# Attention over 4096 memory slots: the value matmuls on fp16 parts in place of fp32r parts

## The reference

```python
q = x @ Wq.T + bq
scores = einsum('bshd,hmd->bshm', q, memory_keys) / sqrt(128)
probs = softmax(scores, axis=-1)                 # over 4096 slots
mem_out = einsum('bshm,hmd->bshd', probs, memory_values)
x = layernorm(x + mem_out @ Wo.T + bo)
h = silu(x @ w1.T * s1) * (x @ w2.T * s2)
h = gelu(h @ h1.T * s_h1); h = gelu(h @ h2.T * s_h2)
out = layernorm(x + h @ w3.T * s3)
```

## Time and profile before

| | |
|---|---|
| median of 3 runs | 1188.73 us (1188.07 to 1192.92) |
| the profiled execution | 1189.26 us |
| its span, first to last instruction | 1187.5 us |
| attention block | until about 803 us |
| feed-forward block | the rest, some 384 us |
| mean granted TensorE clock | 0.978 |

### The profile page before, as it was taken

The page is one execution under the profiler, slowest core; times in us unless marked ns, Lnnn a source line. Parts: engine busy times, 40 slices in busy tenths (PEclk is TensorE's granted clock), DMA queues, the critical chain, the costliest instruction groups (busy, mean ns, idle before and its releaser), DMA issues. The chain is left out here.

```text
span 1187.5 us, 20054 instructions
## 1 busy us (share of the span) xinstructions
PE 1117.8 (94%) x5312; PEld 908.0 (76%) x5312; DVE 968.2 (82%) x1757; ACT 892.6 (75%) x1574; POOL 730.1 (61%) x612
## 2 busy tenths in 40 slices
PE   7799999999999999999999999753999999999996
PEld 6588788888888888888888887532688888888885
DVE  5888888888888888898898898464678878888875
ACT  5677787787878778787877877612788788888883
POOL 4388798889889888888888898882011112112110
PEclk9999999999999999999999999885999999999999
DMA  4878888888888888888888888812000100101000
GB/s 168 200 172 196 184 194 195 192 196 192 198 189 193 199 188 195 199 192 189 199 192 189 198 194 184 218 53 75 19 27 28 54 26 26 53 26 35 28 10 26
DMA packets 81922, 162.96 MB, mean 137 GB/s; under 512 B 19296, under 2 KB 44768, under 8 KB 81888
## 3 DMA queue, kind: packets, MB, share of 16 engines
q1 hardware_dynamic: 81888, 162.55, 57.5%
HBM read 19.87 MB, written 8.39 MB: 24 GB/s over the span
## 5 line engine op out<-in xcount | busy, mean ns | idle before, releaser
L259 POOL TENSOR_TENSOR pT<-slot_p,pT 128x512 fp32r<-128x512 f32 x512 | 653.4, 1314 | 108.8 <-ACT pT L298 108.8
L448 PE MATMUL o_ps<-pT,v_hi 128*128 128x512 f32 x1024 | 392.9, 406 | 21.6 <-POOL pT L259 21.0
L373 DVE TENSOR_SCALAR_CACHE_REDUCE rows<-s_ps 128x1024 f32<-128x1024 f32 x256 | 313.2, 1224 | 86.2 <-PE s_ps L421 77.0
L298 ACT ACTIVATE pT<-slot_p 128x512 fp32r<-128x512 f32 x512 | 297.5, 618 | 102.2 <-DMA slot_p<-rows 62.1
L342 DVE STREAM_TRANSPOSE rows<-rows 128x1024 f32<-128x1024 f32 x256 | 317.2, 1240 | 2.9 <-ACT rows L289 2.7
L289 ACT ACTIVATE rows<-rows,bias 128x1024 f32<-128x1024 f32 x256 | 292.3, 1142 | 9.0 <-DVE bias L379 6.2
L450 PE MATMUL o_ps<-pT,v_lo 128*128 128x256 f32 x1024 | 289.0, 282 | 0.0
L448 PEld LDWEIGHTS o_ps<-pT,v_hi 128*128 128x128 f32 x1024 | 195.1, 191 | 89.7 <-POOL pT L259 44.3
L419 PE MATMUL s_ps<-keys,q_buf 128*128 128x512 f32 x512 | 210.8, 412 | 9.7 <-DVE keys L169 5.2
L450 PEld LDWEIGHTS o_ps<-pT,v_lo 128*128 128x128 f32 x1024 | 195.8, 191 | 18.8
L798 PE MATMUL ring<-h_hi,keys 128*128 128x512 f32 x512 | 203.8, 398 | 1.9 <-DVE h_lo L705 1.6
(11 more groups left out here) (71 smaller groups left out, 1028.4 us busy)
## 6 DMA issues: line engine op xcount, KB each, us to landing
slot_p<-rows SPq DMA_DIRECT2D x1024, 128.0 KB, 2.3
x_in<-in_xT SPq DMA_DIRECT2D x32, 128.0 KB, 2.1
o_scratch<-o_sum SPq DMA_DIRECT2D x32, 128.0 KB, 1.9
o_in<-o_scratch SPq DMA_DIRECT2D x16, 256.0 KB, 2.8
x_in<-in_x SPq DMA_DIRECT2D x16, 256.0 KB, 3.1
out<-y_out SPq DMA_DIRECT2D x16, 256.0 KB, 2.3
slot_p<-in_kT SPq DMA_DIRECT2D x4, 512.0 KB, 6.1
slot_p<-in_vT SPq DMA_DIRECT2D x4, 512.0 KB, 9.2
```

Of the source, the lines that this page charges most:

```text
L259: nc.gpsimd.tensor_tensor(halves(s % RING, 1), slots_first(pp, s), halves(s % RING, 0).bitcast(FP32), ALU.subtract).then_inc(split, 1)
L298: nc.scalar.activation(halves(s % RING, 0), slots_first(pp, s), ACT.Copy).then_inc(highed, 1)
L373: nc.vector.tensor_scalar(row_piece(tile, k), s_ps[:, j % 2, :], 1.0, None, ALU.mult, ALU.max, accum_out=part_max[:, tile, k:k + 1]).then_ ...
L448: nc.tensor.matmul(o_ps[:, pp, :], v_hi[:, 2 * s + c, :], pT[:, s % RING, c, :], start=first, stop=False, skip_group_check=True)
```

## The change

`v_hi`, `v_lo` and `pT` become fp16. The values are multiplied by a power of two, so that fp16 can hold them: their largest magnitude is found on the chip, DVE by pieces of 1024 columns (`v_piece_max`), POOL across partitions, DVE turns it into `v_scale` and `v_unscale`. ACT copies the values to `v_raw` only, in frame 0; in steps 8 to 15 of frame 1 it writes the scaled `v_hi` and then scales `v_raw` in place. PE takes the two `v_lo` matmuls next to each other. The output is scaled back in the two instructions that form `o_sum`. The score matmuls and the feed-forward block stay as they are. The core of the diff:

```diff
-        v_hi = sb("v_hi", [P, SLOTS // P, P], FP32R)
-        v_lo = sb("v_lo", [P, SLOTS // P, P], FP32R)
+        v_hi = sb("v_hi", [P, SLOTS // P, P], FP16)
+        v_lo = sb("v_lo", [P, SLOTS // P, P], FP16)
...
-        pT = sb("pT", [P, RING, 2, 4 * P], FP32R)
+        pT = sb("pT", [P, RING, 2, 4 * P], FP16)
...
+            nc.gpsimd.memset(v_row_max[:, PIECES:PIECES + 1], V_LEAST).then_inc(v_least_ready, 1)
+            pool.wait_ge(v_row_maxed, PIECES + 1)
+            nc.gpsimd.partition_all_reduce(v_max[:, 0:1], v_row_max[:, PIECES + 1:], P, bass.bass_isa.ReduceOp.max).then_inc(v_maxed, 1)
             for n in range(HALVES):
                 pool.wait_ge(v_high, n + 1)
-                pool.wait_ge(v_copied, n + 1)
-                nc.gpsimd.tensor_tensor(half_piece(v_lo_flat, n), half_piece(v_raw, n), half_piece(v_hi_flat, n).bitcast(FP32),
+                pool.wait_ge(v_scaled, n + 1)
+                nc.gpsimd.tensor_tensor(half_piece(v_lo_flat, n), half_piece(v_raw, n), half_piece(v_hi_flat, n),
                                         ALU.subtract).then_inc(v_split, 1)
...
-                        nc.scalar.activation(half_piece(v_hi_flat, n), o_ps[:, n % 2, :], ACT.Copy).then_inc(v_high, 1)
...
+                    if is_step(f, 1) and t >= STEPS - HALVES:
+                        n = t - (STEPS - HALVES)
+                        if n == 0:
+                            act.wait_ge(v_scale_ready, 2)
+                        nc.scalar.activation(half_piece(v_hi_flat, n), half_piece(v_raw, n), ACT.Copy,
+                                             scale=v_scale[:, :]).then_inc(v_high, 1)
+                        act.wait_ge(v_high, n + 1)
+                        nc.scalar.activation(half_piece(v_raw, n), half_piece(v_raw, n), ACT.Copy,
+                                             scale=v_scale[:, :]).then_inc(v_scaled, 1)
...
+            def v_piece_max(n):
+
+                dve.wait_ge(v_copied, 2 * n + 2)
+                nc.vector.reduce_max(v_row_max[:, n:n + 1], piece(v_raw, n), AX.X, apply_absolute_value=True).then_inc(v_row_maxed, 1)
...
+                    if is_step(f, 0) and j > PIECES:
+                        v_piece_max(j - PIECES - 1)
+                    if is_step(f, 1) and j == 0:
+                        v_piece_max(PIECES - 1)
...
+                    if is_step(f, 1) and j == 3:
+                        dve.wait_ge(v_maxed, 1)
...
-                            if is_step(p, 0):
-                                pe.wait_ge(v_split, HALVES)
+                        if is_step(p, 0) and s % 2 == 0:
+                            pe.wait_ge(v_split, s // 2 + 1)
+                        nc.tensor.matmul(o_ps[:, pp, :], v_hi[:, 2 * s, :], pT[:, s % RING, 0, :],
+                                         start=s == 0, stop=False, skip_group_check=True)
                         for c in range(2):
...
+                            nc.tensor.matmul(o_ps[:, pp, 0:2 * P], v_lo[:, 2 * s + c, :], pT[:, s % RING, c, 0:2 * P],
+                                             start=False, stop=False, skip_group_check=True)
+                        nc.tensor.matmul(o_ps[:, pp, :], v_hi[:, 2 * s + 1, :], pT[:, s % RING, 1, :],
+                                         start=False, stop=s == STEPS - 1, skip_group_check=True).then_inc(pv_done, 1)
```

More of the change, by code:

```diff
@@ L22 @@
 FP16 = mybir.dt.float16
+I32 = mybir.dt.int32
 ALU = mybir.AluOpType
@@ L43 @@
 PV_LAG = 16
+V_TOP = 2.0 ** 14
+V_LEAST = 2.0 ** -100
 RING = 8
@@ L106, in attention @@
         table_spare = sb("exp_table_spare", [P, 1], FP32)
+        v_row_max = sb("v_row_max", [P, PIECES + 2], FP32)
+        v_max = sb("v_max", [P, 2], FP32)
+        v_scale = sb("v_scale", [P, 1], FP32)
+        v_unscale = sb("v_unscale", [P, 1], FP32)
         spare_half = slot_p[:, 1, :, :, :].rearrange("p a c t -> p (a c t)")
@@ L321, in frame @@
                         at_least(act, o_ready, f - 3)
-                        nc.scalar.activation(o_tmp[:, :], o_ps[:, 1 - par, 2 * P:], ACT.Copy).then_inc(o_half, 1)
+                        nc.scalar.activation(o_tmp[:, :], o_ps[:, 1 - par, 2 * P:], ACT.Copy,
+                                             scale=v_unscale[:, :]).then_inc(o_half, 1)
             frames(act, frame)
@@ L387, in frame @@
                         at_least(dve, o_stored, 16 * (f - 3))
-                        nc.vector.tensor_tensor(o_sum[:, :], o_ps[:, 1 - par, 0:2 * P], o_tmp[:, :], ALU.add).then_inc(o_ready, 1)
+                        nc.vector.scalar_tensor_tensor(out=o_sum[:, :], in0=o_ps[:, 1 - par, 0:2 * P], scalar=v_unscale[:, :],
+                                                       in1=o_tmp[:, :], op0=ALU.mult, op1=ALU.add).then_inc(o_ready, 1)
             frames(dve, frame)
```

14 lines of the change are left out of this document (13 added, 1 removed).

## The result

The changed kernel took **1183.32 us** (median of 5 runs, 1182.24 to 1185.02), the kernel before 1188.73 us beside it: a ratio of 0.9946, 95% interval 0.9928 to 0.9964. It is 5.4 us faster, on the other side of "no change" from the forecast of 1196, and inside the wide range of 1179 to 1213. The profiled execution of the changed kernel took 1182.86 us, 1180.9 of it the span.

The account below looks back on a forecast made before the run. The prediction took the double buffer between SP's exchange and POOL's subtraction as the bound, not PE. Late start +12.5 and PE's fp16 matmuls -5 gave +7.5 on 1188.73, so 1196 us; range 1179 to 1213.

Parts of the forecast that it names:

- The bound: Attention block: a closed loop of SP's exchange and POOL's subtraction, 46.11 us, sets two frames, not PE.
- with fp16 in and out: I take no change: POOL's 512 low-part subtractions stay at 1.257 us each; bounds 10% either way, about 16 us.
- the text's own sign of being wrong: POOL's low part, expected near 1.26 us, away from that by over 0.05 would show the forecast wrong.
- The rival that named it: POOL's subtraction is quicker on fp16: at 10% less, -16 us, 1180 us; chance 13%.
- The sensitivity: Each 0.1 us on POOL's subtraction moves the kernel 13 us: 10 in the loops, 3 in the last two pairs.
- The count of seven in the loop: Seven of POOL's low parts lie in the loop: one before PE's free run, six after the gap.
- the drain: The last two pairs, 32 subtractions, run at POOL's pace; priced as unchanged.
- The late start: Value preparation before the loop: pair 2's exchange starts 12.5 us late and the loop keeps it; bounds 9 and 15.
- the 5.65 us of preparation: POOL's preparation before the reduction over partitions, taken to stand ahead of the wait for DVE; reduction counted at 0.4 us.
- PE's share: Value matmuls in fp16: a group takes 0.645 us, seven groups save 0.38 us a loop; -5 us, bounds 0 and -8.
- The order of the matmuls: Reorder of the two `v_lo` matmuls on PE: priced at nothing, since no wait names it.

Follow-up runs that it names:

- the constant scale: The changed kernel with the scale fixed at 256, no search for the largest value, values scaled while copied out of PSUM in frame 0: 1170.65 us, ratio 0.9847.
- the mirror image: The kernel before, fp32r matmuls kept, but POOL's subtraction reads one operand in fp16 and writes fp16 into an unread tile: 1178.93 us, ratio 0.9909.
- the early start: The changed kernel with the values' unscaled copy in its own tile and their low parts made half by GpSimd, half by VectorE: 1178.25 us, ratio 0.9900.
- the last run: As the early start, but VectorE makes all eight low parts of the values and GpSimd none: 1177.06 us, ratio 0.9911 to the kernel before.

## Why the prediction was wrong

**The bound was right.** Not PE at 94% but the double buffer between exchange and subtraction sets the frame: it still closes to 0.03 us, a transfer more on SP lengthens it, and 0.12 us off POOL's instruction moves the kernel by 11.7 us.

**The step that failed is POOL's subtraction "with fp16 in and out: I take no change".** The instruction went from 1.257 to 1.13 us, 10% less, which was the text's own sign of being wrong (away from 1.26 by over 0.05). The rival that named it said 16 us less and 1180; the runs show 11.7 less (1194.99 to 1183.32), and 1183. It was there at 13%, and the range holds the result only because it took in half of that rival. The reasoning under the term was half a test: that fp32r written beside fp32 read costs nothing told of the write only, and the write is indeed free. The read was never in the trace, and it is the read that counts. The sensitivity, 13 us for each 0.1 us, was worked out and used only for the range. It was also too high: 0.12 us gave 11.7. The count of seven in the loop nearly holds (0.76 us a loop, 7 x 0.12 = 0.84); but for the drain it took the 32 subtractions of the last two pairs, where only pair 31's sixteen are left outside the loops. In a closed loop such a term should have been carried by its bounds, not by a single value.

The page cited there, of the Trainium skill ("GPSIMD Engine Reference", Instruction dispatch), with both inputs held to one port at some 2.5 cycles an element, was read as leaving the time alone when one input is halved. As a floor it stands: 512 elements at 2.5 cycles and the 1.2 GHz that the page gives are 1.07 us (an estimate from the page's figures), and both measured times lie above that. It has nothing on the size of an element, and what was read out of it is wrong: the time fell from 1.25 to 1.13 us. Nor do the bytes account for it in proportion: a quarter of the input's bytes gone took a tenth of the time.

**The late start was nearly right, in part by luck.** Scale ready at 45.3 (46.8 predicted), a pair of scaled copies every 1.38 us (46.71 - 45.33; 1.38 predicted), POOL free at 62.06 (63.6), the reduction without the 5.65 us of preparation. Pair 2 is 11.3 late against 12.5. But the 12.5 priced the preparation alone, and that is 13.5 (109.95 against 96.49 with the constant scale); 2.2 came back because the rest of the start was quicker than before, which the forecast had not priced. No frame absorbs it; the constant scale gives back 12.7 us.

**PE's share was right.** 0.36 us a loop in PE's free run (0.38 predicted), a value group of 0.66 us (8.81 less six score groups of 0.70, over seven) where 0.645 was predicted. With POOL as before, the loop is 45.78 instead of 46.11, so 0.33; times 14.5 that is 4.8 us, with 0.65 more in pair 31's run (27.60 for 28.25). The forecast had 5. Some 1 us of it may be POOL's: its ten subtractions in a row take 12.45 us in that run and 12.57 before. The order of the matmuls was priced at nothing, and is worth nothing.

**The drain** was not "at POOL's pace": sixteen subtractions of 1.257 are 20.1 us, and pair 31's run took 28.25, with three of them held beside VectorE. The hold is much alike in both kernels and so drops out of their difference.

The sum with the measured terms: +11.3 late start, -4.8 and -0.7 from PE, and from POOL 14.5 x (45.78 - 45.02) = -11.0 in the loop and 27.60 - 25.81 = -1.8 in pair 31. That is -7.0; the spans differ by -6.6. Without POOL's two terms it is +5.8, which the run with POOL as before measured as +6.2. In the other order, POOL alone is worth 9.9 us (the mirror image) and then PE is the bound at 45.5 us; PE's fp16 lowers that bound, and the loop goes on to 45.02.

## What to carry to other kernels

When a data type changes, list every instruction that reads the tile, not only the ones that the change is for, and ask for each what stands in the loop that sets the time; a tenth on a subtraction here outweighed the faster matmuls two to one. Where the trace has no row for a type, a term with a large factor should be carried as a range, or measured by itself first. Work that is done once, before a loop with no slack starts, costs nearly its full lateness (13.5 us here, 12.7 in the time), and it pays to ask what the change has freed (here SBUF) that lets the loop start earlier.

## What the runs showed of the hardware

- GpSimd's subtraction of 512 elements a partition, fp32 with fp16: 1.13 us; fp32 with fp32: 1.25 us; whether it writes fp16 or fp32r makes no difference (five take 5.67 and 5.63 us with the fp16 read, 6.26 and 6.26 with fp32). Its product with a scalar, fp32 read and written, took 1.55 us for the same 512, though it reads one tile only.
- **VectorE and GpSimd hold each other up** where VectorE has an instruction with two SBUF tiles as input, and at the end of the block also its CAST, which reads one. In the early start VectorE's subtraction took 6.99 us instead of 0.74, while GpSimd subtractions ran at their usual pace (the second to the seventh of the seven in a row); in the mirror image the CAST took 10.30 instead of 3.21. In other executions they took turns, with GpSimd's subtractions up to 4.00 us beside the CAST, and up to 1.61 beside VectorE's of 1.59 and 1.64 in the last run. That they took turns there isn't due to gaps in GpSimd's queue, which had none from 58.90 to 69.21:

```profile
58.90 10.31 POOL L266 TENSOR_TENSOR pT<-slot_p,pT 128x512 f16<-128x512 f32 x8 [1.24 <-ACT pT L305]
```

What decides between the two isn't shown. The Trainium skill ("GPSIMD Engine Reference", Specifications) lists this contention for VectorE instructions with two SBUF inputs; the subtraction's rows agree, and show its price. VectorE's transposes and moves of one tile, beside POOL all through the kernel, stay at their 1.2 us.
- A weight load of 128 columns took 95 ns in fp16 (the row of L489 above); the fp32r ones of the scores in the same kernel took 192:

```profile
L462 PEld LDWEIGHTS s_ps<-keys,q_buf 128*128 128x128 f32 x512 | 98.3, 192 | 22.7 <-DVE rows L399 9.8
```

They lie beside the matmuls, and no gain shows that can be put down to them.
- The late start costs clock too. In the windows from 50 to 60 and 60 to 70 us of the changed kernel (columns as above) PE is busy for 2.56 and 6.73 us, and the granted clock is 0.67 and 0.58, a mixture of its two levels; from 70 us on it is 1.00:

```profile
50.00:60.00 10.00, 2.56 (x8) 1.56 (x7) 5.22 (x9) 9.87 (x16) 5.57 (x5) 0.67 0.15 34
60.00:70.00 10.00, 6.73 (x23) 3.94 (x24) 2.44 (x4) 9.97 (x19) 9.27 (x10) 0.58 0.59 141
```

Ahead of it PE waits 10.70 us for POOL (the row at 63.27). With the constant scale the granted clock is 0.83 from 50 to 60 us and 1.00 from 60 to 70, as in the kernel before. What the lower level cost by itself was not measured; a part of the 13.5 us may be its price.
